# A different order of TensorE's slots in a fused delta-rule attention and mixture-of-experts kernel, and the first join of its triangular inverse in four column groups

## The reference

```python
for i in range(3):
    kS = einsum('bhd,bhde->bhe', k_i, S)
    S = S + b_i * (k_i * (v_i - kS))
o = einsum('bhd,bhde->bhe', q, S)
```

## Time and profile before

| | us |
|---|---|
| median of 3 runs (lowest 8217.16, highest 8226.03) | 8217.32 |
| the profiled execution's own time | 8217.97 |
| its span in the profile | 8215.9 |
| PE busy | 7423.3 (90%) |
| PE's weight loads busy | 6296.7 (77%) |
| DVE busy | 6459.2 (79%) |
| ACT busy | 5469.5 (67%) |
| POOL busy | 4117.8 (50%) |

### The profile page before, as it was taken

How to read it: one execution, slowest core, us unless ns; L and a number is a source line. 1 busy time by engine, 2 the same in 40 slices (tenths; PEclk the granted TensorE clock), 3 DMA queues, 4 the chain that set the end, 5 groups by cost and what they waited for, 6 DMA issues and landing times. The chain is left out here.

```text
span 8215.9 us, 426591 instructions
## 1 busy us (share of the span) xinstructions
PE 7423.3 (90%) x155940; PEld 6296.7 (77%) x155940; DVE 6459.2 (79%) x22300; ACT 5469.5 (67%) x20343; POOL 4117.8 (50%) x6333
## 2 busy tenths in 40 slices
PE   5889999999999999999999899999989999889999
PEld 3777777777787777777777777777777777757777
DVE  4888888888888888888888888888888888623333
ACT  3777777777777777777777777777777777533333
POOL 0555555555555555555555555555555555511111
PEclk6899999999999999999999999999999999889999
DMA  2000000000000000000000000000000000010000
GB/s 90 8 10 9 10 9 10 9 10 9 10 10 9 10 10 10 9 10 9 10 9 10 9 10 9 10 9 10 10 9 10 9 10 10 7 32 8 10 8 8
DMA packets 283626, 97.69 MB, mean 12 GB/s; under 512 B 226097, under 2 KB 276545, under 8 KB 281153
## 3 DMA queue, kind: packets, MB, share of 16 engines
q1 hardware_dynamic: 281408, 68.93, 3.8%
HBM read 52.08 MB, written 16.78 MB: 8 GB/s over the span
## 5 line engine op out<-in xcount | busy, mean ns | idle before, releaser
L819 DVE SCALAR_TENSOR_TENSOR CY<-PP,CWV,CY 128x128 f32<-128x128 f32 x4608 | 1585.5, 344 | 148.6 <-ACT CY L736 68.7
L819 DVE SCALAR_TENSOR_TENSOR CY<-PP,CWK,CY 128x128 f32<-128x128 f32 x4608 | 1581.4, 343 | 98.0 <-ACT CY L736 24.3
L1031 POOL TENSOR_TENSOR UM<-U,C 32x256 f32<-32x256 f32 x1536 | 1104.8, 719 | 120.2 <-POOL UM L1031 19.6
L1024 POOL TENSOR_TENSOR Y<-U,C 32x256 f32<-32x256 f32 x768 | 554.0, 721 | 1075.6 <-DVE UQ L912 1035.4
L550 PE MATMUL PI<-T,WB 32*32 32x32 f32 x49152 | 749.6, 196 | 303.2 <-DVE T L828 301.1
L550 PEld LDWEIGHTS PI<-T,WB 32*32 32x32 f32 x49152 | 639.0, 111 | 466.3 <-issue 403.2
L530 PE MATMUL PP<-XT,WV 128*128 128x131 f32 x3072 | 750.8, 328 | 188.5 <-issue 124.7
L530 PE MATMUL PP<-XT,WK 128*128 128x131 f32 x3072 | 783.6, 340 | 81.3 <-DVE CY L819 81.2
L736 ACT ACTIVATE CY<-PP,CWK 128x128 f32<-128x128 f32 x1536 | 564.4, 367 | 398.5 <-PE PP L530 387.4
L1004 POOL TENSOR_TENSOR S<-R,BETA 96x4 f32<-96x4 f32 x512 | 101.3, 198 | 1392.4 <-DVE R L872 1392.2
L736 ACT ACTIVATE CY<-PP,CWV 128x128 f32<-128x128 f32 x1536 | 567.2, 369 | 339.3 <-PE PP L530 328.0
(11 more groups left out here) (228 smaller groups left out, 18910.8 us busy)
## 6 DMA issues: line engine op xcount, KB each, us to landing
EX<-exd SPq DMA_DIRECT2D x768, 32.0 KB
exd<-EXS SPq DMA_DIRECT2D x16, 512.0 KB, 2.6
XR<-in_L_attn_x SPq DMA_DIRECT2D x65, 64.0 KB, 3.1
XL<-in_L_attn_x SPq DMA_DIRECT2D x16, 256.0 KB, 2.8
XRES<-in_L_attn_x SPq DMA_DIRECT2D x64, 64.0 KB, 2.7
x<-X SPq DMA_DIRECT2D x64, 64.0 KB, 3.1
XI<-x SPq DMA_DIRECT2D x16, 256.0 KB, 2.9
out<-OUT SPq DMA_DIRECT2D x16, 256.0 KB, 2.3
```

The source lines that it names most:

```text
L819: dve.scalar_tensor_tensor(CY[:, m % RING], ptile(m)[:, s:s + P], taps_of(m)[:, s:s + 1], CY[:, m % RING], ALU.mult, ALU.add).then_inc(tap ...
L1024: pool.tensor_tensor(Y1[r, :, :], U[r, par, :, r], over(first[r, :], [BK, NHEAD, BK], 1), ALU.mult).then_inc(seed_sb, 1)
L1031: pool.tensor_tensor(UM[r, lv], U[r, par, :, r], over(merge[lv][r, :], [BK, NHEAD, BK], 1), ALU.mult).then_inc(made, 1)
```

## The change

Only PE's order, the first join's place in PSUM and its eviction on ACT change. The programs of DVE, POOL and SP stay as they are.

- The first join writes `mids` (32 columns per head) in column groups 1 and 0 in turn by head, and `his` (64 columns per head) in groups 2 and 3, where both had one group each before. ACT evicts it with four instructions for two.
- Inverse steps 0, 1, 3, 4, 6 stay at the head of their slots. Steps 2, 5 and 7 (`INV_LAST`: slots 4, 10 and 13) go to the end of their slots.
- The corner goes to the head of slot 6, right behind step 3. The second join stays at the end of slot 4, now right behind step 2.
- The read-out goes from slot 11 to slot 10, right behind step 5.
- The first gate part (c = 3) goes to the head of slot 8, behind step 4; the second stays at the end of slot 10, now behind the read-out.

```diff
--- before.py
+++ after.py
@@ -27,6 +27,8 @@
 LH = 4
 STEPS = 8
 INV_AT = {1: 0, 3: 1, 4: 2, 6: 3, 8: 4, 10: 5, 12: 6, 13: 7}
+INV_LAST = (4, 10, 13)
+INV_FIRST = [k for k in INV_AT if k not in INV_LAST]
 
 
 PBANK, CLOSE = [0, 1], (19, 53)
@@ -423,6 +425,8 @@
         inv = PI[0:R, 0:NHEAD * BK].rearrange("p (h c) -> p h c", h=NHEAD)
         join = PB[0:R, :].rearrange("p (h c) -> p h c", h=NHEAD)
         corner = PB[:, 0:4 * BK].rearrange("p (g c) -> p g c", g=2)
+        mids = PB[:, 0:4 * BK].rearrange("p (q c) -> p q c", q=4)
+        his = PB[:, 0:8 * BK].rearrange("p (q c) -> p q c", q=4)
         quad = PB[:, :].rearrange("p (h c) -> p h c", h=4)
         ptile = lambda m: PP[:, PBANK[m], 0:HALO + P]
         row_bank = lambda l, h: (PA, PK)[l][0:R, h % LH]
@@ -636,8 +640,30 @@
                     gate_now = c == 3 and known(i - 1, 0, NSC)
                     next_x = c == 3 and known(i + 1, 1, NSC)
                     for k in range(SLOTS):
-                        if do_inv and k in INV_AT:
+                        if do_inv and k in INV_FIRST:
                             invert(invn, 1 - par, INV_AT[k])
+                        if k == 6 and do_run:
+                            pe.wait_ge(join_sb, 3 * run + 2)
+                            pe.wait_ge(diag_sb, NBK * (run + 1))
+                            for h in range(NHEAD):
+                                j = h % LH
+                                mm = pe.matmul(corner[CT * j:CT * j + CT, h // LH], GA[:, h, 0:BK], YF[:, h, BK:R], start=True, stop=True)
+                            mm.then_inc(join_ps, 1)
+                        if k == 8 and gate_now:
+                            l = 0
+                            if l == 0:
+                                if do_run:
+                                    pe.wait_ge(join_sb, 3 * run + 3)
+                                if known(i - 2, 0, NSC):
+                                    pe.wait_ge(y_sb, i - 1)
+                            else:
+                                pe.wait_ge(gsil_sb, 2 * (i - 1) + 1)
+                            wg = WG[:, :].rearrange("p (g j d) -> p g j d", g=2, j=LH)
+                            for cc in range(2):
+                                t0 = HALO + CT * (2 * l + cc)
+                                for j in range(LH):
+                                    mm = pe.matmul(quad[CT * j:CT * j + CT, 2 * cc:2 * cc + 2], XT[:, 1 - half, t0:t0 + CT], wg[:, :, j], start=True, stop=True)
+                            mm.then_inc(gate_ps, 1)
                         if known(i, 0, NSC):
                             project(i, half, SLOTS * c + k)
                         if k in (1, 4) and do_run:
@@ -649,29 +675,15 @@
                             side_bank_free(i, c, run, do_run)
                             mid, hi = slice(BK, 2 * BK), slice(2 * BK, R)
                             for h in range(NHEAD):
-                                pe.matmul(join[mid, h, 0:BK], U[:, par, h, mid], X3[:, h, 0:BK], start=True, stop=True)
-                                mm = pe.matmul(join[hi, h], U[:, par, h, hi], X3[:, h], start=True, stop=True)
-                            mm.then_inc(join_ps, 1)
-                        if k == 4 and do_run:
-                            pe.wait_ge(join_sb, 3 * run + 1)
-                            pe.sem_inc(begun, 1)
-                            hi = slice(2 * BK, R)
-                            for h in range(NHEAD):
-                                mm = pe.matmul(join[BK:2 * BK, h, 0:BK], GA[hi, h, BK:2 * BK], Y3[hi, h], start=True, stop=True)
-                            mm.then_inc(join_ps, 1)
-                        if k == 6 and do_run:
-                            pe.wait_ge(join_sb, 3 * run + 2)
-                            pe.wait_ge(diag_sb, NBK * (run + 1))
-                            for h in range(NHEAD):
-                                j = h % LH
-                                mm = pe.matmul(corner[CT * j:CT * j + CT, h // LH], GA[:, h, 0:BK], YF[:, h, BK:R], start=True, stop=True)
+                                q, o = h // 2, 1 - h % 2
+                                pe.matmul(mids[CT * o:CT * o + CT, q], U[:, par, h, mid], X3[:, h, 0:BK], start=True, stop=True)
+                                o = 2 + h % 2
+                                mm = pe.matmul(his[CT * o:CT * o + CT, q], U[:, par, h, hi], X3[:, h], start=True, stop=True)
                             mm.then_inc(join_ps, 1)
                         if k in (7, 9) and do_prep:
                             gram(k // 9, c, sc, prep)
                         if k in (8, 9) and do_run:
                             solve(k - 8, run, prep, do_prep)
-                        if k == 11 and do_run:
-                            read_out(run, rc)
                         if k in (10, 11) and do_run:
                             new_state(k - 10, run, rc, prep, do_prep)
                         if k in (12, 13) and do_prep:
@@ -688,8 +700,28 @@
                             for h in range(LH):
                                 mm = pe.transpose(quad[:, h], OG[:, 2 * l + h // 2, h % 2], ident)
                             mm.then_inc(ogt_ps, 1)
-                        if k in (8, 10) and gate_now:
-                            l = (k - 8) // 2
+                        if k == 12 and out_now:
+                            pe.wait_ge(ogt_sb, 2 * (i - 1))
+                            for h in range(NHEAD):
+                                mm = pe.matmul(PB[:, 0:P], OGT[:, h], WO[:, h], start=(h == 0), stop=(h == NHEAD - 1))
+                            mm.then_inc(wo_ps, 1)
+                        if k == 12 and next_x:
+                            if gate_now:
+                                pe.wait_ge(gsil_sb, 2 * i)
+                            transpose_x(i + 1, 1 - half)
+                        if do_inv and k in INV_LAST:
+                            invert(invn, 1 - par, INV_AT[k])
+                        if k == 4 and do_run:
+                            pe.wait_ge(join_sb, 3 * run + 1)
+                            pe.sem_inc(begun, 1)
+                            hi = slice(2 * BK, R)
+                            for h in range(NHEAD):
+                                mm = pe.matmul(join[BK:2 * BK, h, 0:BK], GA[hi, h, BK:2 * BK], Y3[hi, h], start=True, stop=True)
+                            mm.then_inc(join_ps, 1)
+                        if k == 10 and do_run:
+                            read_out(run, rc)
+                        if k == 10 and gate_now:
+                            l = 1
                             if l == 0:
                                 if do_run:
                                     pe.wait_ge(join_sb, 3 * run + 3)
@@ -703,15 +735,6 @@
                                 for j in range(LH):
                                     mm = pe.matmul(quad[CT * j:CT * j + CT, 2 * cc:2 * cc + 2], XT[:, 1 - half, t0:t0 + CT], wg[:, :, j], start=True, stop=True)
                             mm.then_inc(gate_ps, 1)
-                        if k == 12 and out_now:
-                            pe.wait_ge(ogt_sb, 2 * (i - 1))
-                            for h in range(NHEAD):
-                                mm = pe.matmul(PB[:, 0:P], OGT[:, h], WO[:, h], start=(h == 0), stop=(h == NHEAD - 1))
-                            mm.then_inc(wo_ps, 1)
-                        if k == 12 and next_x:
-                            if gate_now:
-                                pe.wait_ge(gsil_sb, 2 * i)
-                            transpose_x(i + 1, 1 - half)
 
                 pe.wait_ge(ready, READY)
                 transpose_x(0, 0)
@@ -750,8 +773,12 @@
                             op.then_inc(sso_sb, 1)
                         if k == 2 and do_run:
                             act.wait_ge(join_ps, 3 * run + 1)
-                            act.activation(GA[BK:2 * BK, :, 0:BK], join[BK:2 * BK, :, 0:BK], ACT.Copy, scale=-1.0)
-                            act.activation(GA[2 * BK:R], join[2 * BK:R], ACT.Copy, scale=-1.0).then_inc(join_sb, 1)
+                            for e in range(2):
+                                o = CT * (1 - e)
+                                act.activation(GA[BK:2 * BK, e:NHEAD:2, 0:BK], mids[o:o + CT], ACT.Copy, scale=-1.0)
+                                o = CT * (2 + e)
+                                op = act.activation(GA[2 * BK:R, e:NHEAD:2], his[o:o + CT], ACT.Copy, scale=-1.0)
+                            op.then_inc(join_sb, 1)
                         if k == 4 and do_run:
                             act.wait_ge(join_ps, 3 * run + 2)
                             need(act, z_ps, 2 * run)
```

## The result

The changed kernel takes 8671.3 us (8665.8 to 8688.5), the one before 8221.7 (8217.2 to 8250.8): a ratio of 1.056, interval 1.053 to 1.058, 450 us slower. Forecast was 8355, 133 us more than the kernel before: the sign was right, the size under a third of what was measured, and 8671 lies outside the range of 8165 to 8450.

What follows compares the result with a forecast made beforehand. PE and DVE, both nearly full, were taken to hand the lead over in a ring, neither bounding alone. +4.6 us per eight chunks, times 32, gave +147, taken as 140 on 8217, about 8355; range 8165 to 8450.

Steps and rivals of the forecast that it cites:

- Slot 10 and the c = 1 chunk: Slot 10: new state 0 waits for ACT's eviction, delaying step 5 and DVE; +1.25 us per c = 1 chunk, bounds 0.4 to 1.7.
- PE's savings end in a wait: Slot 7: PE finishes the corner early and waits for DVE at projection 7, so its savings so far gain nothing.
- Join and step 2: First join falls from 1.02 to 0.58 us; in slot 4 the later step 2 makes DVE lose 0.37.
- the 0.1 booked for it: Borders between full and tiled products: about 0.1 us at entry, 0.1 in the next full group, another 0.1 on leaving.
- Wait of projection 7: Slot 7: the projection waits for DVE over 1 us.
- c = 2: the step that failed: Chunks with the output part: wait before step 2 shrinks from 2.28 to about 1.9; +0.1 if the clock falls, -2.3 if held, mean -1.1.
- the sum: Eight chunks, one loop turn: 2 x 1.55 + 2 x 1.25 + 2 x 0.6 - 2 x 1.1 = +4.6 us.
- that walk: c = 2 chunk with the clock held: second solve 3.3 us earlier, step 5 1.2, step 6 3.0, step 7 2.3, so -2.3.
- c = 0 and c = 3: c = 0: +1.55 us, 0.3 of it for less PE waiting at K's transposes; c = 3, with the gate: +0.6.
- the 1.7 of step 5: c = 3: step 5 comes 1.7 us later, but DVE's waits of 0.57 at step 6 and 0.53 for transposed x close: +0.6.
- PE as the bound: Rival 3, whole attention part: PE bounds and the new-state wait costs nothing, so faster, 7900 or likelier 8080; chance 0.22.
- The drop of the clock in every c = 2 chunk (8440): Rival 2: PE's clock falls each time at c = 2, +0.1 us per such chunk, +224 in all, 8440; chance 0.15.

Runs made afterwards that it cites:

- the changed kernel with spare work: The changed kernel plus two never-read products ahead of slot 1's projection and two ahead of new state 0 in slot 10: 8592.0 us, ratio 1.048.

## Why the prediction was right and wrong

**Slot 10 and the c = 1 chunk: right, shown.** Forecast: new state 0 waits 0.5 to 0.9 behind ACT's eviction, DVE 1.2 to 1.7, slot 12's wait gone, 25.1 us. Measured 0.55, 1.77, gone, 25.20 in the chunk shown and 25.1 and 25.2 in the mean with the clock held. That PE's savings end in a wait was right too. That they cost nothing there was not: by the run with the join alone, that longer wait lowers the clock.

**Join and step 2: right.** The join takes 0.58 as forecast (4056.57 to the start of step 1 at 4057.15), DVE waits 0.31 at step 2 for 0.37 forecast. From its start to its neighbour's, step 2 beside the second join takes 0.60 instead of 0.63; step 3 ahead of the corner and step 5 ahead of the read-out keep 0.63 (full clock, nearly all chunks). That agrees in direction with what the Trainium skill (TensorEngine Tiling (Array Packing), Tiling Modes) says on a change of mode and the prediction weighed. But 0.03 is less than the 0.1 booked for it, and no row shows the border at no cost.

**Wait of projection 7: too large.** I had over 1 us for it; at c = 1 it is about 0.4, with 0.62 already at projection 5 (4062.68).

**c = 2: the step that failed.** I booked a mean of -1.1 per chunk, half of them without a fall, and +0.1 for those with it. Measured +0.9 and +1.8: of the 9.95 us per turn that the sum lacks, 5.0 are here, against 2.5 at c = 3, 1.5 at c = 0 and 1.0 at c = 1. The wait was indeed shorter, 1.57 at the projection of slot 4, but it is followed by 0.91 ahead of the projection of slot 7 and 1.04 ahead of step 4, and the clock falls there (in 38 of the 60 c = 2 chunks between 11.3 and 12.8 us from their start; here at 4093.49):

```profile
4085.47 0.49 PE L534 MATMUL PP<-XT,WK 128*128 128x131 f32 x2 [1.57 <-DVE CY L846]
...
4090.82 0.49 PE L534 MATMUL PP<-XT,WK 128*128 128x131 f32 x2 [0.91 <-DVE CY L846]
4091.14 1.04 PE L583 MATMUL PK<-KQ 128*96 128x128 f32 x8
4093.22 1.22 PE L552 MATMUL PI<-XB,UM 32*32 32x32 f32 x48 [1.04 <-issue]
4094.37 0.81 PE L534 MATMUL PP<-XT,WK 128*128 128x131 f32 x2
4094.97 1.91 PE L594 MATMUL PA<-BZ,YF 96*96 96x128 f32 x8
```

That is the stretch in which PE leads; before, it fell in slot 4, where DVE's own work covered part. I looked at one wait and not at all that the new order opens. No c = 2 chunk of the changed kernel is without time at half clock, so the half of them booked at -2.3 never came. Nor was that walk right for a held clock: 29.2 by the forecast (31.46 - 2.3), 30.0 in the changed kernel with spare work. Before the change such a chunk is 28.8, so with the clock held the change costs 1.2 here too.

**Falls elsewhere: left out.** Outside c = 2 and the seam the kernel before has almost none; the changed one has them in all chunks (5.6 per turn in sum). At c = 1 they make the whole difference between the 1.25 forecast, right where the clock holds, and the +1.8 and +1.7 of the means. By the estimate above, half clock costs 3.8 us more per turn than before; the sum had nothing for it outside c = 2, and there a gain.

**c = 0 and c = 3: mis-sized.** At c = 0, +1.55 was forecast and +2.6 and +2.0 came, +1.8 with the clock held: step 5 late alone gives 1.3 to 1.4, and 0.5 goes when step 2 is put back at the head (0.3 booked). At c = 3, +0.6 was forecast and +1.6 and +2.1 came, +1.15 with the clock held. I let the 1.7 of step 5 close two DVE waits in full. With step 5 alone late, DVE waits 1.06 at step 6 all the same, and the chunk grows by 2.1; the neighbours give 0.9 of it back (26.6 for 27.5 with all steps at the heads).

**Rivals.** PE as the bound is out: the join alone would have gained 113 us, and lost 414 against the 8240.3 measured beside it. The drop of the clock in every c = 2 chunk (8440) was the nearest to the 8671 measured, and its condition came true, but it priced such a chunk at +0.1.

## What to carry to other kernels

When two engines hand the lead to each other, find for each moved instruction what stood behind it and hid a third engine's latency: here one step, moved behind a projection and one group of products, uncovered a 0.6 us eviction and by itself cost 375 to 396 us; put back, it took 302 of the 450 us away. The parts do not add up, since each change moves waits and with them the clock: compare chunks with the clock held, and the time at half clock, each for itself. Work saved on an engine that waits anyway only lengthens the wait; look at its clock before and after. A few spare products in such a wait gained 1.9%, more than any order of the real work here; no order without spare work beat the kernel before.

## What the hardware showed

A shorter program part cost 5%: 0.44 us less PE work per chunk took the mean granted clock from 0.95 to 0.87 and the time from 8240 to 8654, and four spare products, 1.1 us of PE's time, in the same wait brought it to 8224 (clock 0.96). In the kernel before, the clock falls in 54 of 60 c = 2 chunks. The wait at step 2 is 2.28 to 2.30 in all 60, so its length alone does not decide. The falls cost 2.0 to 2.5 us per c = 2 chunk (31.3 and 30.9 in the mean, 28.8 in the six without a fall). All this is measured in this kernel alone.
